# A graph kernel's setup in another order, with the node features loaded as soon as the edge list is stored

## The reference

```python
msg = x[src] + edge_attr
agg = jax.ops.segment_sum(msg, dst, num_segments=N)
h = jax.nn.relu(agg @ W1 + b1) @ W2 + b2
mu = jnp.mean(h)
var = jnp.mean((h - mu) ** 2)
h = (h - mu) * jax.lax.rsqrt(var + EPS) * ln_w + ln_b
mean = jnp.mean(h, axis=0)
sub = h - gn_ms * mean
gvar = jnp.mean(sub ** 2, axis=0)
h = sub * jax.lax.rsqrt(gvar + EPS) * gn_w + gn_b
h = jax.nn.gelu(h)
x = _layernorm(x + (h + x), axis=-1)
```

## Time and profile before

| | us |
|---|---|
| median of 3 runs (lowest to highest) | 753.34 (753.02 to 753.58) |
| the profiled execution | 756.05 |
| its span in the profile | 754.2 |
| PE, DVE, ACT, POOL busy | 691.8, 631.5, 424.5, 115.1 |

### The profile page before, as it was taken

The page is one execution under the profiler, slowest core; times in us unless marked ns, Lnnn a source line. Parts: engine busy times, 40 slices in busy tenths (PEclk is TensorE's granted clock), DMA queues, the critical chain, the costliest instruction groups (busy, mean ns, idle before and its releaser), DMA issues.

```text
span 754.2 us, 25355 instructions
## 1 busy us (share of the span) xinstructions
PE 691.8 (92%) x9473; PEld 628.4 (83%) x9473; DVE 631.5 (84%) x1067; ACT 424.5 (56%) x962; POOL 115.1 (15%) x90
## 2 busy tenths in 40 slices
PE   0976899999999999999999999999999999999963
PEld 0965789988899888998899988999889998888842
DVE  4786989889899898998989989899898998835576
ACT  0943565466655666457564566646665466614447
POOL 2042301110011101111011110211101110100024
PEclk9995799999999999999999999999999999999996
DMA  6957535466354662556625665356553565400006
GB/s 136 329 191 220 182 99 198 152 219 209 88 190 170 214 209 71 196 185 212 196 74 187 206 208 172 100 179 217 189 172 119 177 219 172 144 16 0 0 1 170
DMA packets 87489, 120.41 MB, mean 160 GB/s; under 512 B 8718, under 2 KB 84486, under 8 KB 87267
## 3 DMA queue, kind: packets, MB, share of 16 engines
q1 hardware_dynamic: 80724, 113.10, 46.6%
q0 software_dynamic: 5744, 5.38, 2.7%
q10 hardware_dynamic: 1000, 1.65, 0.9%
HBM read 116.03 MB, written 4.03 MB: 159 GB/s over the span
## 4 chain that ended last, share of the span: by engine, by line
PE 76%; ACT 9%; DVE 5%; DMA 4%; issue 3%; POOL 1%; ACTq 0%; DVEq 0%; POOLq 0%; SPq 0%
PE bank L832 40%; PE bank L774 18%; PE bank L722 10%; ACT counts L609 6%; PE bank L876 3%; PE bank L866 3%; PE bank L736 2%; ACT below L553 2%; DMA begins<-listed,tile_slot 2%; DMA agg<-in_dst_dram 1%; DMA near<-listed,row_slot 1%; POOL pool_m L526 1%; DVE x_lo L1059 1%; PE bank L751 1%; DVE pool_m L1118 1%
## 5 line engine op out<-in xcount | busy, mean ns | idle before, releaser
L609 ACT CAST counts<-bank 128x490 fp32r<-128x490 f32 x600 | 320.1, 605 | 239.0 <-PE bank L774 236.1
L832 PE MATMUL bank<-counts,x_hi 128*128 128x250 f32 x1225 | 308.7, 291 | 8.5 <-ACT counts L609 8.4
L832 PE MATMUL bank<-counts,x_lo 128*128 128x250 f32 x1225 | 293.2, 279 | 0.0
L832 PEld LDWEIGHTS bank<-counts,x_hi 128*128 128x128 f32 x1225 | 231.1, 189 | 14.8 <-ACT counts L609 14.0
L1118 DVE TENSOR_TENSOR pool_m<-value_row,turned_lo 128x3328 bf16<-128x3328 bf16 (+1 forms) x125 | 229.1, 1833 | 12.1 <-PE bank L774 11.6
L832 PEld LDWEIGHTS bank<-counts,x_lo 128*128 128x128 f32 x1225 | 232.3, 190 | 0.0
L774 PE MATMUL bank<-pool_m 128*128 128x98 bf16 x3125 | 196.0, 211 | 8.6 <-DVE pool_m L1118 8.6
L774 PEld LDWEIGHTS bank<-pool_m 128*128 128x128 bf16 x3125 | 159.6, 99 | 28.3 <-issue 12.8
L1118 DVE TENSOR_TENSOR pool_m<-value_row,turned_key 128x2548 bf16<-128x2548 bf16 (+1 forms) x125 | 179.7, 1437 | 0.0
L486 POOL DMA_INDIRECT near<-listed,row_slot x27 | 53.6, 1986 | 501.6 <-DVE row_slot L1080 460.0
L722 PE MATMUL bank<-edges,onehot 128*32 128x128 f32 x3228 | 121.6, 284 | 5.9 <-DMA edges<-in_edge_attr_dram 3.9
(11 more groups left out here) (156 smaller groups left out, 461.7 us busy)
## 6 DMA issues: line engine op xcount, KB each, us to landing
edges<-in_edge_attr_dram SPq DMA_DIRECT2D x134, 768.0 KB
out_dram<-pool_m SPq DMA_DIRECT2D x12, 256.0 KB
agg<-in_dst_dram SPq DMA_DIRECT2D x1, 768.0 KB
agg<-in_src_dram ACTq DMA_DIRECT2D x1, 768.0 KB
listed<-agg ACTq DMA_DIRECT2D x1, 768.0 KB
begins<-listed,tile_slot POOLq DMA_INDIRECT x28, 4.2
near<-listed,row_slot POOLq DMA_INDIRECT x27
pool_m<-in_L_gnn_W_dram SPq DMA_DIRECT2D x2, 128.0 KB, 2.2
```

What stands on the lines that cost most here:

```text
L609: nc.scalar.copy(counts[:, :, at:at + NODES], cps[k % RING][:, 0:NODES * NT].rearrange("p (n q) -> p q n", q=NT)).then_inc(banks_free, 1)
L832: last = nc.tensor.matmul(sps[:, 0:CHUNK], part[:, q, :], counts[:, q, at:at + CHUNK], start=(q == 0 and part is x_hi), stop=(q == NT - 1 ...
```

## The change

The order of the setup is another on every engine, and x gets a place of its own.

- x is loaded into `x_in`, which lies where `x_lo` is, no longer into `pool_m`; `x_lo` is written over it in place. So marks can be made in `pool_m` while x is on its way.
- SP issues the `dst` loads with the small ones first and waits for no pad; the pad is written elsewhere and POOL copies it into `rows_i` by a DMA. x is issued when the whole list is stored (`listed_stored`), as POOL's first gather is, and the edges after it. ACT's `src` loads have the small ones first, too.
- POOL issues `begins` of chunk 1 ahead of the zeroing of `agg`.
- ACT copies the keys and the first six banks before it copies x and the lead sums.
- PE turns the keys within the last search, after four of its seven sets, then counts six banks, then does the lead groups.
- DVE stages row 0 before the destinations are turned into columns; takes the words of chunk 0 before any lead group, makes marks 0 and 1, then the one-hots of groups 0 and 1, marks 2, the words of chunk 1, splits x, groups 2 and 3, marks 3.

The diff without parts that only move a definition:

```diff
+        x_in = nc.alloc_sbuf_tensor_at("x_in", [P, NT, D], F32, offset=x_lo_at)
...
+        pad_row = x_raw[0:1, 0:GROUP - REST].bitcast(I32)
...
@@ block.sync
-            sp.dma_start(rows_i[0:EVEN, :], dst_full[0:EVEN, :]).then_inc(dst_loaded, 16)
-            sp.wait_ge(rows_padded, 2)
             sp.dma_start(rows_i[EVEN:FULL, :], dst_full[EVEN:FULL, :]).then_inc(dst_loaded, 16)
             sp.dma_start(rows_i[FULL:GROUPS, 0:REST], dst_rest).then_inc(dst_loaded, 16)
-            sp.wait_ge(src_loaded, 48)
+            sp.dma_start(rows_i[0:EVEN, :], dst_full[0:EVEN, :]).then_inc(dst_loaded, 16)
             sp.wait_ge(rows_padded, 3)
-            sp.dma_start(x_raw[:, 0:(NT - 1) * D].rearrange("p (t d) -> p t d", d=D),
...
-            sp.dma_start(x_raw[0:LAST, (NT - 1) * D:NT * D], x[(NT - 1) * P:N, :]).then_inc(x_loaded, 16)
+            sp.wait_ge(listed_stored, 64)
+            sp.dma_start(x_in[:, 0:NT - 1, :], x[0:(NT - 1) * P, :].rearrange("(t p) d -> p t d", p=P)).then_inc(x_loaded, 16)
+            sp.dma_start(x_in[0:LAST, NT - 1, :], x[(NT - 1) * P:N, :]).then_inc(x_loaded, 16)
@@ block.gpsimd
+            pool.wait_ge(rows_padded, 2)
+            pool.dma_start(rows_i[FULL:GROUPS, REST:GROUP], pad_row).then_inc(pad_loaded, 16)
...
             gather_begins(0)
             gather_near(0)
+            gather_begins(1)
             pool.wait_ge(turned, TURNS)
             pool.memset(agg[:, :], 0.0).then_inc(agg_zeroed, 1)
             with pool.Fori(1, CHUNKS + 2) as c:
-                gather_begins(c)
                 gather_near(c)
-            gather_begins(CHUNKS + 2)
+                gather_begins(c + 1)
@@ block.scalar
+            act.wait_ge(pads_ready, 1)
+            copy_keys(0)
+            count_cover(0)
             for k in range(AHEAD):
                 copy_bank(0, k, 0)
+            act.wait_ge(x_loaded, 32)
+            for i in range(NT // PIECE):
+                at = slice(i * PIECE, (i + 1) * PIECE)
+                nc.scalar.copy(x_hi[:, at, :], x_in[:, at, :]).then_inc(x_high, 1)
+            for g in range(LEAD):
+                copy_sums(g, g % GPC)
             count_cover(1)
@@ block.tensor
-            search(2)
-            lead_groups(0)
+            search(2, range(SETS // 2 + 1))
             turn_keys(0)
-            lead_groups(GPC)
-            turn_sums(LEAD - 1, (LEAD - 1) % GPC)
+            search(2, range(SETS // 2 + 1, SETS))
...
+            for k in range(COUNTED):
+                if k == RING - 1:
+                    pe.wait_ge(tiles_read, 2)
+                count_bank(0, k)
+            lead_groups(0)
+            lead_groups(GPC)
+            turn_sums(LEAD - 1, (LEAD - 1) % GPC)
             pe.wait_ge(x_split, NT // PIECE)
-            for k in range(COUNTED):
-                count_bank(0, k)
@@ block.vector
+            dve.wait_ge(pad_loaded, 16)
...
             dve.engine_nop().then_inc(rows_ready, 1)
+            stage_row(0)
...
+            split_words(0)
+            widen_words(0)
+            join_keys(0)
+            stage_tile(1)
+            dve.wait_ge(pads_ready, 1)
+            mark_batch(0, 0)
+            dve.wait_ge(below_used, len(PIECES) * SETS)
+            read_tiles(PIECES[1][0], CHUNKS, signs=True)
+            dve.engine_nop().then_inc(tiles_read, 1)
+            mark_batch(0, 1)
+            stage_row(1)
             for g in range(GPC):
                 mark_lead(g, 0)
                 mark_lead(g, 1)
                 if g == 0:
                     put(g)
-            stage_row(0)
+            mark_batch(0, 2)
+            split_words(1)
+            widen_words(1)
+            join_keys(1)
+            stage_tile(2)
             for i in range(NT // PIECE):
                 split_x(i)
-            split_words(0)
...
             dve.wait_ge(agg_zeroed, 1)
             for g in range(GPC, LEAD):
                 mark_lead(g, 0)
                 add(g - GPC, g % GPC, base_of(g - GPC))
                 put(g - 1)
                 mark_lead(g, 1)
-            dve.wait_ge(below_used, len(PIECES) * SETS)
...
+            stage_row(2)
+            stage_tile(3)
+            mark_batch(0, 3)
             mark_pair(0, 0)
             add(LEAD - 2, 0, base_of(LEAD - 2))
             put(LEAD - 1)
             add(LEAD - 1, 1, base_of(LEAD - 1))
-            mark_batch(0, 1)
...
             mark_pair(0, 1)
             mark_pair(0, 2)
-            mark_batch(0, 2)
-            stage_row(2)
-            stage_tile(3)
-            mark_batch(0, 3)
```

More of the change, by code:

```diff
@@ L563, in _ @@
             search(2)
-            act.wait_ge(x_loaded, 32)
-            for i in range(NT // PIECE):
-                at = slice(i * PIECE, (i + 1) * PIECE)
-                nc.scalar.copy(x_hi[:, at, :], x_raw[:, i * PIECE * D:(i + 1) * PIECE * D].rearrange("p (t d) -> p t d", d=D)
-                               ).then_inc(x_high, 1)
             def copy_sums(g, s):
@@ L596, in count_cover @@
                                      ).then_inc(cover_counted, 1)
-            for g in range(LEAD):
-                if g == GPC:
-                    act.wait_ge(pads_ready, 1)
-                    copy_keys(0)
-                    count_cover(0)
-                copy_sums(g, g % GPC)
             def copy_bank(c, k, odd):
@@ L682, in _, with search @@
         def _(pe):
-            def search(piece):
+            def search(piece, sets=range(SETS)):
                 a, b = PIECES[piece]
-                for i in range(SETS):
+                for i in sets:
                     n = piece * SETS + i
@@ L975, in stage_tile, with prep_chain, stage_row @@
                 dve.tensor_copy(tile_slot[0:PAIRS, :], tile_rows[0:PAIRS, bass.ds(c, 1)]).then_inc(tile_staged, 1)
+            def prep_chain(ins, count):
+                ins.then_inc(prep, 1)
+                dve.wait_ge(prep, count)
+            STEPS = 2
+            def stage_row(c):
+                dve.wait_ge(begins_loaded, c * 16 + 16)
+                n = c * STEPS
+                prep_chain(dve.tensor_scalar(begins[0:PAIRS, :].bitcast(F32), begins[0:PAIRS, :], pair_w[0:PAIRS, bass.ds(c, 1)], 0.0,
+                                             ALU.is_lt, ALU.add, accum_out=first_f[0:PAIRS, :]), n + 1)
+                prep_chain(dve.scalar_tensor_tensor(first_i[0:PAIRS, :], tile_f[0:PAIRS, bass.ds(c, 1)], float(SPAN),
+                                                    first_f[0:PAIRS, :], ALU.mult, ALU.add), n + 2)
+                dve.tensor_scalar(row_slot[0:PAIRS, :], first_i[0:PAIRS, :], 4, None, ALU.arith_shift_right
+                                  ).then_inc(row_staged, 1)
             dve.memset(tile_f[:, :], 0.0)
```

36 lines of the change are left out of this document (6 added, 30 removed).

## The result

The changed kernel takes **760.18 us** (median of 4 runs, 759.71 to 761.08), the kernel before in the same runs 753.18 (751.97 to 753.58): ratio 1.0094, 95% interval 1.0078 to 1.0111. It is slower by 7.0 us. The forecast, 755.2, had the sign, but a quarter of the size. The profiled execution of after took 759.71, its span is 757.9.

The account below looks back on a forecast made before the run. PE was taken to bound the loop, DVE the setup: 6.4 us of head start become 0.7 lost, first chunk sum 1.85 later, so 756.05 becomes 757.9; less 2.7 above the median, 755.2. Range 750.8 to 758.8.

Parts of the forecast that it names:

- list stored: SP's store of the list without x in front: done at 23.4 us instead of 27.52, a gain of 4.1; bounds 27.5 and 21.5.
- begins, near landed: POOL's first two gathers: begins beside x takes 11.5 us and lands at 34.9, near takes 6.5 and lands at 43.2.
- first marks: DVE's first marks, after the words and the turned keys: at 45.9 us, 6.4 earlier than 52.30.
- from there to the end of the fifth marks: DVE's stretch of marks: 33.8 us of work, gaps and waits, sum 36.5, ending at 82.4 against 81.70.
- PE free for the banks, before the fifth marks: PE can count banks once the last lead sum is turned, 2.0 us ahead of the fifth marks' start: 77.1.
- from there to the first chunk sum: PE's banks, halves, turns and keys: 9.9 us at the full clock, plus 0.9 for the clock; first chunk sum 87.9.
- The forecast's 1.85: First chunk sum at 87.9 us against 86.05 in the kernel before: 1.85 us later.
- Case (1): Rival: begins gather let in early beside x, costing 8.2 us, landing at 31.6; first marks 2.4 earlier, 752.8; chance 0.24.
- the bound: Limits on the reordered loads' effect on list readiness: from 0.4 us gained to 0.6 lost, 0 taken.
- 2.4 of waits: DVE between first and fifth marks: 0.7 for PE's search, 1.0 for the second near gather, 0.7 for turned sums.
- case (3): Rival, slower by more: second near gather falls behind refilled edges, DVE waits 3.5 more, or PE at half clock; 758.7; chance 0.15.
- 0.9 us for the clock: PE's banks before the first chunk sum: half clock would lose 2.8 us; a third of it, 0.9, was taken.

Follow-up runs that it names:

- e7: Changed kernel with the zeroing ahead of the second begins gather and half the bytes in edge refills from group 4 on: 755.42 against 754.27, ratio 1.0009.
- e4: Changed kernel, but SP issues x, and the edges behind it, only when the first near gather has landed: 757.35 against 754.27, ratio 1.0055.
- e8: Changed kernel with the zeroing of agg at its place, cut into eight pieces: 761.57 against 753.67, ratio 1.0100.
- e6: Changed kernel with x at its old queue place, zeroing ahead of the second begins gather, lead groups 0 and 1 early, x's splitting spread over DVE's waits: ratio 1.0037.
- e11: Changed kernel with x's load waiting for the first near gather and the zeroing ahead of the second begins gather: 759.85 against 753.21, ratio 1.0080.
- e1: Changed kernel, but POOL zeroes agg before it issues begins of chunk 1, as in the kernel before: 757.47 against 753.15, ratio 1.0065.
- e10: e6 plus groups 2 and 3 in DVE's wait for the second near gather and the zeroing in eight pieces: 756.98 against 753.67, ratio 1.0050.
- the kernel before again: The kernel before, unchanged, run for a second profile: 753.11 against 753.15, ratio 1.0002.
- e3: Changed kernel with half the bytes in every refill of an edge half from group 4 on (those sums are wrong): 757.24 against 753.15, ratio 1.0058.
- e9: Changed kernel with groups 2 and 3 marked and added ahead of x's splitting, ACT's copies reordered to match: 763.49 against 753.67, ratio 1.0131.
- e2: Changed kernel, but x is issued at its old place in SP's queue, as soon as src is loaded: 759.84 against 753.15, ratio 1.0080.
- e5: Changed kernel with groups 0 and 1 earlier: one-hots in DVE's wait for the near gather, group 0 summed before the turned keys: 763.42 against 754.27, ratio 1.0131.

## Why the prediction was right or wrong

| us | forecast | measured | adds to the loss |
|---|---|---|---|
| list ready for its store | 17.74 | 16.85 | |
| list stored | 23.4 | 23.15 | |
| begins, near landed | 34.9, 43.2 | 33.90, 42.77 | |
| first marks | 45.9 | 45.44 | -0.46 |
| from there to the end of the fifth marks | 36.5 | 38.55 (to 83.99) | +2.05 |
| PE free for the banks, before the fifth marks | 2.0 | 2.1 (at 78.61) | -0.1 |
| from there to the first chunk sum | 10.8 | 12.92 | +2.12 |
| first chunk sum of the kernel before | 86.05 | 84.54 | +1.51 |

The forecast's 1.85 and the last column give 7.0. So two steps failed: the zeroing was put down as costing DVE nothing, and PE's waits for refilled edges stood at nothing. The reference was 1.5 us off as well. That the sign came out right is in part luck: with the two costs taken away (e7) the time can't be told from the kernel before's (0.9995 to 1.0023), so it is mostly what the sum left out that made the change slower.

**The list and the gathers: right, but for 1 us.** The list's store gains what x in front had cost it, and the first gather beside x is nearly as slow as forecast (10.75 us from the stored list to its landing, against 11.5; POOL issues it only 1.0 after the list is stored, a step that the sum doesn't have, and the 2.9 us in it should by its own rows be 2.7). Of the list's own 7 us behind x the gather got about 5.6 (9.7 instead of 4.1 in e4). Case (1), let in early, would have landed it at 31.6. In the Trainium skill, "DMA: Bandwidth & Descriptors" (Queues, rings and completion order), queues take turns by packets of typically 9 to 17 descriptors, which I had read as a wait of a quarter of the list's; e4 shows some 80% of it. The pad's DMA does land last of the loads, at 13.13, and still the list was ready 0.9 earlier, within reach of the bound.

**DVE from the first to the fifth marks: the lock was missed.** The order of the work holds, and so does the sum of the rest: 32.87 - 2.81 + 3.28 = 33.3 us of work, against 33.8, and 2.4 us idle, against 2.4 of waits plus 0.3 of gaps (all of it for turned sums and in gaps; neither PE's search nor the second near gather was waited for). That the waits agree is luck: the turned sums cost 2.1 us instead of 0.7, the other two nothing instead of 1.7. What failed is the sentence that the zeroing of `agg` "stands ahead of that second near gather, beside marks; it ran beside x's splitting on DVE at no visible cost to either". In the kernel before it had TENSOR_TENSOR beside it, and in after the marks, TENSOR_TENSOR as well, pass unhurt (1.89 and 1.48 us); the TENSOR_SCALAR between them doesn't. And the cost was visible before the change, at the tail of the zeroing (41.47 to 46.91), in a row of DVE that the prediction read only as the start of the words:

```profile
46.32 0.68 DVE L1089 TENSOR_SCALAR lo_i<-near 125x128 int32<-125x128 int32 x1
```

The same instruction takes 0.23 us at 65.98; the 1.65 us for the words hold some 0.4 of this. I costed an overlap by the engine, and not by the kinds of instruction that the new order puts into it. The runs show the hold on three kinds of step, always until 0.03 to 0.15 us after POOL's end: `tile_rows` (2.98 in after, 3.27 in e8), `place` (3.84 in e6), the words (2.77 in e6, 4.50 in e11); e1 takes it away. What is held reads SBUF; what reads a PSUM bank isn't (the TENSOR_SCALAR of 0.17 at 48.64 in after). In the Trainium skill, "SBUF — State Buffer" (Who interferes with whom), just this is told: `tensor_scalar` may enter a mode that takes the ports shared with GpSimd, the one that issues first has them for its whole instruction, and the other blocks. The trace agrees, but in e8 and e10 the hold lasts over eight instructions in a row. I had quoted that section for TENSOR_TENSOR, and asked only whether POOL is held up by DVE; here it is DVE that is held up by POOL. My case (3) named a stall behind the zeroing as its sign, with the roles turned round; its price, 3.5 us, was near.

**PE from the banks to the first chunk sum: the refills were missed.** Its work is 10.18 us, against 9.9, and the clock is full from 77.9 to 83.5, where I took 0.9 us for the clock: that term was zero in this execution. The clock was at half from 63.0 to 73.3 us and full from there through the first chunk sum; PE summed groups 2 and 3 as it rose, from 70.2 to 75.5; in e1, e4 and e7 it fell once more before the banks. The three waits, 2.74 us, stood nowhere. I had written that the second near gather may fall behind refilled edges, but not that PE itself waits for these edges. The rows were there: groups 2 and 3 were marked ahead of the first marks and summed by 58.4 us, and SP asked the first four refills of the loop at 55.6 to 59.8 (56.5 to 60.8 in the kernel before again); the change puts these groups behind x's splitting, and SP asks at 74.5 to 76.8. The views of the DMA engines over 60 to 95 us, in 40 slices, first the kernel before again, then after, with their edge loads (number, KB each, median us to landing), show it: seven loads spread over the 35 us, against eleven, with an idle hole at 69 to 75 us and a crush behind it.

```profile
DMA  9799999983599305698022247996998980002032
...
edges<-in_edge_attr_dram SPq DMA_DIRECT2D x7, 768.0 KB, 5.8
```

```profile
DMA  9979999899610000036999999999999999999999
...
edges<-in_edge_attr_dram SPq DMA_DIRECT2D x11, 768.0 KB, 8.0
```

e3 (smaller refills) and e9 (earlier ones) take these waits away. Of the 0.91 us at 88.33 the profile names no cause. The last of the four refills landed at 88.05, so it is likely the same wait; no row says so. It is gone in e3, where the DMA engines have less to do.

**The baseline: a wrong reference.** I set the forecast against the profiled execution's own time and took its 2.7 us above the median as lying outside the change. Of these, 1.5 lay inside the stretch that the change rewrites (a slower gather, and the full clock 3.2 us later), and the rest in the two chunks behind it; the profile of after shows no such loss behind its first chunk sum but 0.2 us. Against a profile at the median the same steps would have given 87.9 - 84.54 = 3.4 us of loss instead of 1.85, 756.7 us.

**The bound changes hands.** Two chains end at the first chunk sum: DVE's marks, and the refills with PE behind them. Edits that help one can meet the other: e2 brings the fifth marks 2.2 us forward and nothing of it is left at the first chunk sum, with 4.3 us of PE's waits for edges; e6 brings them 5.7 forward and keeps 5.0. The granted clock comes on top, and it wasn't a part of any of my theories:

| run | PE's longest wait while it counts | clock last at half before the first chunk sum | first chunk sum |
|---|---|---|---|
| the kernel before again | 3.26 | 77.0 to 80.4 | 84.54 |
| after | 1.67 | 63.0 to 73.3 | 91.53 |
| e1 | 1.16 | 75.7 to 79.1 | 89.69 |
| e2 | 3.79 | 83.4 to 86.8 | 91.98 |
| e5 | 3.77 | 82.6 to 89.4 | 94.13 |
| e8 | 3.20 | 86.3 to 89.7 | 94.66 |
| e11 | 3.19 | 83.3 to 86.8 | 91.32 |

In the last four the clock falls within that wait or up to 1.1 us behind it, and the banks and halves that follow take up to 1.84 and 1.51 us instead of 1.10 and 0.86: by that, an estimated 1.4 us for 3.4 us at half clock. Together this is why the gains of single edits don't simply add.

**What stays open.** e7 leaves 0.7 us by the times or 2.5 by its profile. The half clock isn't what is left, for it stands in both profiles (74.9 to 78.3 us, and 77.0 to 80.4 in the kernel before again). A likely part, not shown, is PE's backlog: before, PE counted banks while DVE waited; now the last lead groups stand ahead of them (e10's 11.77 us). A kernel in which PE counts first was not run. Nor was a version found that beats the kernel before; the best whole one is at 1.0037.

## What to carry to other kernels

When work is moved beside a long instruction of another engine, list which kinds of instruction will now run beside it; a small one between two harmless ones can be held for all that is left of the long one. Of everything that frees a buffer, ask when its refill was issued before and when it will be now, even if the engine that waits has slack. Where TensorE waits for such a refill, look at the granted clock behind the wait too, for the wait alone isn't the whole cost. And measure where the profiled execution's excess over the median lies before setting a sum against it: a second profile of the unchanged kernel would have given 1.5 us here.

## What the runs showed of the hardware

- A TENSOR_SCALAR of DVE of 0.17 to 0.3 us that reads SBUF, f32 to int32, int32 to int32 and bf16 to f32, waits for the end of a POOL MEMSET that it starts beside (it then takes 0.68 to 4.50 us). TENSOR_TENSOR (bf16 marks, f32 splitting of x) doesn't, nor does a TENSOR_SCALAR that reads a PSUM bank (0.17), nor a small MEMSET of DVE (0.16 at 35.63 in e11). One-hots that stand behind a held TENSOR_SCALAR end with it (e6: 43.05).
- Eight POOL MEMSETs of 0.7 us back to back hold it until the last ends, as one of 5.44 does: it isn't let in between (3.27 us in e8, 4.12 in e10).
- A gather with a 3.2 MB load issued beside it takes 9.7 and 7.1 us from issue to landing, alone 4.1 (e4) and 3.2 (e11).
- 768 KB loads bunched, up to four in flight, land a median of 8.0 us after their issue, spread over time 5.8.
- At half the granted clock 20 matmuls of banks take 1.84 us and 24 of a half of edges 1.51, at the full clock 1.10 and 0.86. Between executions of one kernel the clock can come back 3.2 us later (the two profiles of the kernel before).
